# A new order of all five engines in a period of an attention and pooling kernel, with a fixed PSUM bank for each step

## The chip, the cores and the metric

The kernel runs on one core of one Trainium2 chip. The metric is device microseconds (us) of one execution; lower is better. Engines are named as in the profile: PE is TensorE, DVE is VectorE, ACT is ScalarE, POOL is GpSimd, SP is SyncE, which here only issues DMAs.

## The reference

The input `x` and a side input have 8 batches of 256 rows and 256 columns, in float32. Two layers with residuals follow each other:

```python
# layer 1: 16 heads of 16; keys and values from x; each row of side is also its own key and value
query = side + b_self;  key = [x + b_prev ; side + b_self];  value = [x ; side]
q, k, v = query @ Wq + bq, key @ Wk + bk, value @ Wv + bv
score = [ q.k_prev * s, masked beyond seq_len ; q.k_self * s ]      # 256 scores and one more
w = softmax(score)
x1 = x + (w_prev @ v_prev + w_self * v_self) @ Wo + bo
# layer 2: every row pools over the rows that its kind of mask allows
scores = tanh(x1 @ W1 + b1) @ v
p = softmax(where(mask, scores, -1e30))
out = x1 + (p @ x1) / count(mask)
```

## The kernel before, in words

Every float32 product with a weight is made of three products of float32r parts (`hi x hi`, `hi x lo`, `lo x hi`). So most results leave a PSUM bank twice: ACT copies the high part, DVE subtracts it to get the low part, and only then is the bank free.

The work is a software pipeline over batches. `period(n)` is written for each engine by hand, and each engine runs its own list in order; semaphores alone tie the lists together. In period n, PE works on four batches:

- batch n+1: transposes of side (`TS`, `side_transposed`) and x (`TX`, `x_transposed`), queries (`Q`), two halves of the keys (`K0`, `K1`), self values (`VS`), self scores (`SS`), values (`V`).
- batch n: eight maximum scores (`score_for_max`, two heads each, into `ps_max`), from which DVE takes row maxima (`max_of`), and the first exp scores.
- batch n-1: the other exp scores (`score_for_exp` into `ps_exp`), whose exponentials ACT writes (`exps`), four products of these with the values (`pv`, `PV0` to `PV3`), copied to `o_sb` by ACT, and the transposes back to natural order (`naturals`, `NAT0`, `NAT1`). DVE makes denominators and numerators of them (`denominators`: `den`, `rden`, `num`), and POOL multiplies (`attention`: `attn`).
- batch n-2: the transpose of attention (`AT`), the output product (`WO`), to which DVE adds the residual (`add_residual`: `x1`), the transpose of x1 (`X1T`), the hidden product of the pooling (`Z`, `pool_hidden`), its scores (`SB`), masked by DVE (`masked_scores`), exponentiated by ACT (`pool_exps`: `pool_p`), transposed (`PT`), and the pooled product (`PO`, `pooled`).

`ps_max` and `ps_exp` hold one score block each (two banks of PSUM each): a maximum score waits for the maximum before it (`max_found`), an exp score for the exponentials before it (`p_ready`). The other steps share four banks of `ps_any`. `shared_banks` walks `USES` (lines 43 to 67) and hands the banks out in rotation, in the order of use; `take_bank` (L1022) makes PE wait until the bank's last reader is done.

The row maxima reach the exp scores through a chain of small steps: DVE negates and splits them (`group_max`), PE transposes them (`max_to_rows`, `MT0` and `MT1` for heads 0 to 7 and 8 to 15), ACT copies the rows (`max_rows_copy`: `mt_sb`), and SP places them into `q_rows` by DMA (`place_max`, L335). Exp score 0 waits for group 0 and exp score 4 for group 1. Queries and keys take a longer way: they are spilled to DRAM (`spill_q`, `spill_k`) and read back by rows (`place_q`, `place_k`, in two groups); maximum score 0 of the next batch waits for group 0 of both.

In a period of before, PE's list has eight slots. Each has one maximum score, one exp score and, in every second one, a `pv`; the other steps stand between the slots. Lines 1214 to 1272 have PE's list, 629 to 677 ACT's, 931 to 976 DVE's, 474 to 487 POOL's and 384 to 400 SP's. SP's list is also hand-made: loads of x and side two batches ahead, spills and placements of batch n+1, and the residual's second load of x. Before the first period, batch 0 and the side, x and queries of batch 1 are prepared.

## Time and profile before

| | us |
|---|---|
| median of 3 runs | 306.69 |
| lowest and highest | 303.89, 310.06 |
| the profiled execution, its own time | 307.28 |
| its span, first to last instruction | 305.5 |

The profiled execution has busy shares of its span of 78% on PE, 58% on DVE, 50% on ACT and 21% on POOL. A busy share counts a matmul from its start to its modelled end, and those overlap, so start-to-start distances tell what a step takes on PE. DMA queues moved 35.57 MB at a mean of 116 GB/s. A row of waits names the waiting engine, the tile it works on, the engine and line that released it, and the time. PEclk is the clock granted to PE, 1.00 at 2.4 GHz and 0.50 at 1.2 GHz.

### The profile page before, as it was taken

The numbers are of one execution on the slowest core, as the hardware profiler recorded it, in microseconds if no ns is written. First come the engines' busy times: TensorE is split into PE (matmuls) and PEld (weight loads), VectorE is DVE, ScalarE is ACT, GpSimd is POOL, SyncE is SP. The second block draws the span as 40 slices with busy tenths as digits, with TensorE's granted clock in tenths as the row PEclk, the third lists the DMA queues.
The fourth block names the chain that finished last, engine by engine and source line by source line (L and its number), as shares of the span: only waits on it lengthen the run. The fifth ranks groups of instructions, "written<-read, shape, count | busy, mean of one in ns | idle before, by whom it ended". The sixth has DMA issues, their size and how long they took to land.

```text
span 305.5 us, 5479 instructions
## 1 busy us (share of the span) xinstructions
PE 238.5 (78%) x1988; PEld 180.8 (59%) x1988; DVE 178.4 (58%) x367; ACT 152.5 (50%) x281; POOL 64.8 (21%) x80
## 2 busy tenths in 40 slices
PE   2667487798888988898889888888898788586433
PEld 1657366566665767576757675766576546264323
DVE  3763547656766577657765776576658486214431
ACT  4133114566655656565656565656565274553220
POOL 9400100030151034103410341034104111411400
PEclk9978779799999999999999999999999797779957
DMA  6459615834952854285426542833274110200100
GB/s 164 139 195 208 185 68 146 171 106 163 199 165 101 185 134 141 100 194 128 139 98 176 149 141 92 190 71 124 101 189 79 36 39 2 72 0 0 36 1 34
DMA packets 28283, 35.57 MB, mean 116 GB/s; under 512 B 4440, under 2 KB 24672, under 8 KB 28256
## 3 DMA queue, kind: packets, MB, share of 16 engines
q1 hardware_dynamic: 27616, 33.12, 40.9%
q0 software_dynamic: 640, 2.10, 2.0%
q8 instruction: 16, 0.26, 0.4%
q14 instruction: 11, 0.09, 0.1%
HBM read 20.26 MB, written 14.69 MB: 114 GB/s over the span
## 4 chain that ended last, share of the span: by engine, by line
PE 56%; DVE 15%; issue 11%; ACT 9%; DMA 5%; SPq 2%; POOL 1%; ACTq 0%; DVEq 0%; POOLq 0%
PE ps_any L1013 14%; PE ps_any L1056 9%; PE ps_max L1094 7%; PE ps_any L1120 5%; PE ps_any L1019 5%; PE ps_any L1190 3%; PE ps_exp L1108 3%; PE ps_any L1136 3%; DMA q_rows<-mt_sb 2%; PE ps_any L1167 2%; ACT pool_p L620 2%; DVE s_max L828 2%; DVE prod L814 2%; PE ps_any L1175 2%; ACT q_full L523 2%
## 5 line engine op out<-in xcount | busy, mean ns | idle before, releaser
L828 DVE TENSOR_REDUCE s_max<-ps_max 128x4 f32<-128x1024 f32 x64 | 78.0, 1219 | 37.5 <-PE ps_max L1094 37.4
L542 ACT ACTIVATE pt<-ps_exp 128x1024 f32<-128x1024 f32 x64 | 65.5, 1024 | 52.3 <-PE ps_exp L1108 51.8
L1094 PE MATMUL ps_max<-k_rows,q_rows 49*128 49x256 f32 x256 | 33.1, 338 | 10.0 <-DVE s_max L828 7.5
L1120 PE MATMUL ps_any<-pt,v_aug 128*32 128x256 f32 x512 | 36.3, 403 | 0.3 <-ACT pt L542 0.3
L437 POOL TENSOR_TENSOR attn<-num,rden 128x256 f32<-128x256 f32 x16 | 9.6, 623 | 113.7 <-DVE rden L871 113.7
L1108 PE MATMUL ps_exp<-q_rows,k_rows 51*128 51x256 f32 x256 | 27.9, 296 | 6.4 <-DMA q_rows<-mt_sb 5.8
L1094 PEld LDWEIGHTS ps_max<-k_rows,q_rows 49*128 49x128 f32 x256 | 19.8, 190 | 22.0 <-DVE s_max L828 10.3
L1108 PEld LDWEIGHTS ps_exp<-q_rows,k_rows 51*128 51x128 f32 x256 | 20.4, 192 | 8.8 <-DMA q_rows<-mt_sb 7.1
L423 POOL TENSOR_TENSOR q_lo<-q_full,q_hi 128x512 fp32r<-128x512 f32 x7 | 8.9, 1274 | 74.9 <-ACT q_hi L528 74.9
L1013 PE MATMUL ps_any<-w_hi,in_hi 128*128 128x256 f32 x64 | 21.2, 331 | 3.0 <-DVE w_lo L710 2.6
L1120 PEld LDWEIGHTS ps_any<-pt,v_aug 128*32 128x32 f32 x512 | 13.8, 112 | 11.1 <-issue 2.1
L1013 PE MATMUL ps_any<-w_lo,in_hi 128*128 128x256 f32 x64 | 18.5, 290 | 0.0
L1013 PE MATMUL ps_any<-w_hi,in_lo 128*128 128x256 f32 x64 | 18.5, 289 | 0.0
L429 POOL TENSOR_TENSOR x_lo<-x,x_hi 128x512 fp32r<-128x512 f32 x8 | 10.4, 1304 | 31.6 <-ACT x_hi L597 31.6
L535 ACT ACTIVATE k_hi<-ps_any,bqk_col 128x256 fp32r<-128x256 f32 x16 | 7.6, 473 | 17.9 <-PE ps_any L1056 17.9
L1013 PEld LDWEIGHTS ps_any<-w_hi,in_hi 128*128 128x128 f32 x64 | 12.6, 196 | 6.6 <-issue 5.5
L1013 PE MATMUL ps_any<-w_hi,at_hi 128*128 128x256 f32 x32 | 10.9, 340 | 5.1 <-DVE at_lo L875 5.1
L1056 PE MATMUL ps_any<-in_hi,w_hi 128*128 128x512 f32 x32 | 14.8, 461 | 0.0
L1190 PE MATMUL ps_any<-x_hi,pool_pt_hi 128*128 128x256 f32 x32 | 10.3, 323 | 5.5 <-ACT v_aug L583 3.4
L795 DVE TENSOR_TENSOR in_lo<-ps_any,in_hi 128x512 fp32r<-128x512 f32 x8 | 5.5, 692 | 14.7 <-ACT in_hi L496 14.7
L548 ACT ACTIVATE o_sb<-ps_any 128x256 f32<-128x256 f32 x32 | 12.3, 384 | 3.3 <-PE ps_any L1120 3.3
L1056 PE MATMUL ps_any<-in_hi,w_lo 128*128 128x512 f32 x32 | 13.8, 431 | 0.0
(136 smaller groups left out, 535.8 us busy)
## 6 DMA issues: line engine op xcount, KB each, us to landing
q_rows<-q_spill SPq DMA_DIRECT2D x32, 192.0 KB, 4.3
k_rows<-k_spill SPq DMA_DIRECT2D x32, 192.0 KB
q_spill<-q_hi SPq DMA_DIRECT2D x16, 256.0 KB, 2.5
k_spill<-k_hi SPq DMA_DIRECT2D x16, 256.0 KB, 2.5
s_sb<-in_fside_BxSxS SPq DMA_DIRECT2D x8, 256.0 KB, 6.2
x_sb<-in_x SPq DMA_DIRECT2D x8, 256.0 KB, 5.9
q_spill<-q_lo SPq DMA_DIRECT2D x8, 256.0 KB, 2.7
k_spill<-k_lo SPq DMA_DIRECT2D x8, 256.0 KB, 2.1
```

The source lines that it names most:

```text
L429: nc.gpsimd.tensor_tensor(x1_lo[:], x1[:], x1_hi[:].bitcast(F32), ALU.subtract).then_inc(x1_lo_done, 1)
L437: nc.gpsimd.tensor_tensor(attn[:, t].rearrange("p (h d) -> p h d", d=DH), num[:, t].rearrange("p (h d) -> p h d", d=DH), rden[:, t].unsque ...
L542: nc.scalar.activation(pt[:, 2 * j % 8:2 * j % 8 + 2], ps_exp[:], ACT.Exp).then_inc(p_ready, 1)
L548: nc.scalar.activation(o_sb[:, g], bank_of(f"PV{g}", b)[:, 0], ACT.Copy).then_inc(pv_copied, 1)
L828: nc.vector.tensor_reduce(s_max[:, j // MJ, :, j % MJ, :], ps_max[:], AX.X, ALU.max).then_inc(max_found, 1)
L1013: last = pe.matmul(out_of[:, m], lhs, rhs, start=(j == 0), stop=(j == len(terms) - 1))
L1019: last = pe.transpose(out_of[:, kb, P * t:P * t + P], src[:, t, P * kb:P * kb + P], ident[:])
L1056: last = pe.matmul(bank.rearrange("p w s -> p (w s)"), (w_hi, w_lo)[c][:, 1, kb, P * m:P * m + P], (in_hi, in_lo)[a][:, kb].rearrange("p w ...
L1094: last = pe.matmul(ps_max[:, e, t], q_rows[b % 2][rows, j, P * t:P * t + P], k_rows[b % 2][rows, j, :], start=True, stop=True)
L1108: last = pe.matmul(ps_exp[:, e, t], k_rows[b % 2][rows, j, P * t:P * t + P], q_rows[b % 2][rows, j, :], start=True, stop=True)
L1120: last = pe.matmul(bank[32 * c:32 * c + 32, 0, :], v_aug[b % 2][:, t, h, :], pt[:, h % 8, t, :], start=(t == 0), stop=(t == KB - 1), skip_ ...
L1190: last = pe.matmul(bank[:, t], p[:, kb, P * t:P * t + P], a[:, kb, :], start=(j == 0), stop=(j == len(terms) - 1))
```

## The change

No instruction and no operand changes; the order of the five lists and the assignment of banks do. The steps of one batch also move between periods:

- `USES` has an explicit bank per step, and `shared_banks` follows a list of first uses and then the table. The table's order is PE's new order.
- PE: the output product of n-2 comes right behind maximum score 1. Attention's transpose moves from the period n+2 of a batch n to its period n+1, behind maximum score 7; side is transposed for batch n+2 in place of n+1, late in the period. `pv` 1 and `pv` 2 stand back to back behind exp score 6. One key half stands behind exp score 4, the other behind exp score 5 and the transpose of x1. The naturals come before maximum score 6 in place of behind 7, and exp score 2 of a batch moves to the end of its own period. Self values, naturals and pooled product are split into halves by argument; self values have `pv` 3 between their halves.
- DVE: products and low keys come before maximum 4 in place of behind it; denominators come between maxima 5 and 6; the side's low part is for batch n+2, and attention's low part ends the list.
- ACT: the order follows PE's; the copy of the second group of maxima rows ends the list of period n, ahead of exps 2 of batch n.
- POOL: attention and residual are for batch n-1, behind the x1 low part; the store comes last.
- SP: the loads are issued a period earlier, and the second group of maxima rows is placed behind both groups of the next batch's rows of q and k. The residual's load stands between these groups.

In the diff, removed lines of the lists of ACT, DVE and PE are left out (they stand above), as are the splits into halves.

```diff
 USES = [
...
+    ("MT1", -1, 2, "mt_copied", 2, 2),
+    ("PV0", -1, 0, "pv_copied", 4, 1),
+    ("TX", 1, 2, "xt_lo", 1, 1),
+    ("Q", 1, 1, "q_full_done", 1, 1),
+    ("WO", -2, 2, "x1_done", 1, 1),
+    ("K0", 1, 3, "k_lo", 2, 1),
+    ("X1T", -2, 0, "x1t_lo", 1, 1),
+    ("K1", 1, 1, "k_lo", 2, 2),
+    ("PV1", -1, 2, "pv_copied", 4, 2),
+    ("PV2", -1, 0, "pv_copied", 4, 3),
+    ("MT0", 0, 3, "mt_copied", 2, 1),
+    ("Z", -2, 1, "tanh_done", 1, 1),
+    ("SS", 1, 2, "ss_copied", 1, 1),
+    ("SB", -2, 1, "masked_done", 2, 2),
+    ("VS", 1, 3, "vs_copied", 1, 1),
+    ("PV3", -1, 2, "pv_copied", 4, 4),
+    ("NAT0", -1, 1, "num_done", 2, 1),
+    ("NAT1", -1, 0, "num_done", 2, 2),
+    ("PT", -2, 2, "pt_lo", 1, 1),
+    ("TS", 2, 3, "st_lo", 1, 1),
+    ("V", 1, 0, "v_copied", 1, 1),
+    ("AT", -1, 1, "at_lo", 1, 1),
+    ("PO", -2, 3, "out_done", 1, 1),
 ]

+FIRST_USES = [("TS", 0), ("TX", 0), ("Q", 0), ("K0", 0), ("K1", 0), ("VS", 0), ("SS", 0), ("V", 0),
+              ("TS", 1), ("TX", 1), ("Q", 1)]
+
 
 def shared_banks():
 
-    free, last, found = [None] * BANKS, -1, {}
-    for period in range(-1, NB + 3):
-        for step, offset, reader, per, done in USES:
-            if not 0 <= period + offset < NB:
-                continue
-            last = (last + 1) % BANKS
-            found[step, period + offset] = (last, free[last], len(found))
-            free[last] = (reader, (period + offset) * per + done)
+    row = {use[0]: use[2:] for use in USES}
+    order = FIRST_USES + [(step, period + offset) for period in range(-1, NB + 4) for step, offset, *_ in USES]
+    free, found = [None] * BANKS, {}
+    for step, b in order:
+        if not 0 <= b < NB or (step, b) in found:
+            continue
+        bank, reader, per, done = row[step]
+        found[step, b] = (bank, free[bank], len(found))
+        free[bank] = (reader, b * per + done)
     return found
...
-            for n in range(B + 1):
-                if live(n + 2):
+            for n in range(B + 2):
+                if 2 <= n + 2 < B:
                     load(n + 2)
+                if 1 <= n < B:
+                    spill_q(n)
+                    spill_k(n)
+                if live(n - 1):
+                    place_max(n - 1, 0)
+                if 1 <= n < B:
+                    place_q(n, 0)
+                    place_k(n, 0)
+                if live(n - 2):
+                    load_residual(n - 2)
+                if 1 <= n < B:
+                    place_q(n, 1)
+                    place_k(n, 1)
                 if live(n - 1):
                     place_max(n - 1, 1)
-                if live(n + 1):
-                    spill_q(n + 1)
-                    spill_k(n + 1)
-                if live(n):
-                    place_max(n, 0)
-                if live(n + 1):
-                    place_q(n + 1, 0)
-                    place_k(n + 1, 0)
-                    place_q(n + 1, 1)
-                    place_k(n + 1, 1)
-                if live(n - 1):
-                    load_residual(n - 1)
...
-            for n in range(B + 3):
-                if live(n - 2):
-                    attention(n - 2)
-                    residual(n - 2)
-                if n == 0:
-                    queries_lo(1)
-                elif live(n + 1):
+            for n in range(B + 2):
+                if 1 <= n + 1 < B:
                     queries_lo(n + 1)
-                if live(n - 3):
-                    store(n - 3)
                 if live(n - 1):
                     self_values(n - 1)
                 if live(n - 2):
                     x1_low(n - 2)
+                if live(n - 1):
+                    attention(n - 1)
+                    residual(n - 1)
+                if live(n - 2):
+                    store(n - 2)
             pool.wait_ge(out_stored, 16 * B)
...
         def _(act):
...
             def period(n):
+                if live(n - 1):
+                    exps(n - 1, 2)
+                    pv_copy(n - 1, 0)
+                if 2 <= n + 1 < B:
+                    x_hi(n + 1)
+                if live(n - 1):
+                    exps(n - 1, 3)
+                if 2 <= n + 1 < B:
+                    queries(n + 1)
+                if live(n - 1):
+                    exps(n - 1, 4)
+                    exps(n - 1, 5)
+                if live(n - 2):
+                    x1t_high(n - 2)
+                if 1 <= n + 1 < B:
+                    keys_hi(n + 1)
+                if live(n - 2):
+                    x1_high(n - 2)
+                if live(n - 1):
+                    exps(n - 1, 6)
+                if live(n):
+                    max_rows_copy(n, 0)
+                if live(n - 1):
+                    pv_copy(n - 1, 1)
+                    self_exps(n - 1)
+                if live(n - 2):
+                    tanh(n - 2)
+                if live(n - 1):
+                    exps(n - 1, 7)
+                if 1 <= n + 1 < B:
+                    self_scores_copy(n + 1)
+                if live(n - 1):
+                    pv_copy(n - 1, 2)
+                    pv_copy(n - 1, 3)
+                if live(n - 2):
+                    pool_exps(n - 2)
+                if 1 <= n + 1 < B:
+                    self_values_copy(n + 1)
+                if live(n):
+                    exps(n, 0)
+                if live(n - 2):
+                    pool_high(n - 2)
+                if 2 <= n + 2 < B:
+                    side_hi(n + 2)
+                if live(n):
+                    exps(n, 1)
+                if live(n - 1):
+                    attention_hi(n - 1)
+                if 1 <= n + 1 < B:
+                    values_copy(n + 1)
+                if live(n):
+                    max_rows_copy(n, 1)
 
...
         def _(dve):
...
             def period(n):
+                if live(n):
+                    max_of(n, 0)
+                if live(n - 3):
+                    result(n - 3)
+                if 2 <= n + 1 < B:
+                    x_lo(n + 1)
+                if live(n):
+                    max_of(n, 1)
+                if live(n - 1):
+                    self_args(n - 1)
+                if live(n):
+                    max_of(n, 2)
+                if live(n - 2):
+                    add_residual(n - 2)
+                if live(n):
+                    max_of(n, 3)
+                    group_max(n, 0)
+                if live(n - 2):
+                    x1t_low(n - 2)
+                if 1 <= n + 1 < B:
+                    products(n + 1)
+                    keys_lo(n + 1)
+                if n + 1 == 1:
+                    weight_lo(3)
+                if n + 1 == 1:
+                    output_bias()
+                if live(n):
+                    max_of(n, 4)
+                if live(n - 2):
+                    hide(n - 2)
+                    masked_scores(n - 2)
+                if live(n):
+                    max_of(n, 5)
+                if live(n - 1):
+                    denominators(n - 1)
+                if live(n):
+                    max_of(n, 6)
+                if live(n - 2):
+                    pool_low(n - 2)
+                if 2 <= n + 2 < B:
+                    side_lo(n + 2)
+                if live(n):
+                    max_of(n, 7)
+                    group_max(n, 1)
                 if n == 0:
+                    setup_pooling()
+                if live(n - 1):
+                    attention_lo(n - 1)
 
...
         def _(pe):
...
             def period(n):
+                if live(n):
+                    score_for_max(n, 0)
+                if live(n - 1):
+                    max_to_rows(n - 1, 1)
+                    pv(n - 1, 0)
+                if 2 <= n + 1 < B:
+                    x_transposed(n + 1)
+                    queries(n + 1)
+                if live(n):
+                    score_for_max(n, 1)
+                if live(n - 1):
+                    score_for_exp(n - 1, 3)
+                if live(n - 2):
+                    output_product(n - 2)
+                if live(n):
+                    score_for_max(n, 2)
+                if live(n - 1):
+                    score_for_exp(n - 1, 4)
+                if 1 <= n + 1 < B:
+                    keys(n + 1, 0)
+                if live(n):
+                    score_for_max(n, 3)
+                if live(n - 1):
+                    score_for_exp(n - 1, 5)
+                if live(n - 2):
+                    x1_transposed(n - 2)
+                if 1 <= n + 1 < B:
+                    keys(n + 1, 1)
+                if n + 1 == 1:
                     bv_product()
+                if live(n):
+                    score_for_max(n, 4)
+                if live(n - 1):
+                    score_for_exp(n - 1, 6)
+                    pv(n - 1, 1)
+                    pv(n - 1, 2)
+                if live(n):
+                    max_to_rows(n, 0)
+                if live(n - 2):
+                    pool_hidden(n - 2)
+                if live(n - 1):
+                    score_for_exp(n - 1, 7)
+                if live(n):
+                    score_for_max(n, 5)
+                if 1 <= n + 1 < B:
+                    self_scores(n + 1)
+                if live(n - 2):
+                    pool_scores(n - 2)
+                if 1 <= n + 1 < B:
+                    self_values(n + 1, 0)
+                if live(n - 1):
+                    pv(n - 1, 3)
+                if 1 <= n + 1 < B:
+                    self_values(n + 1, 1)
+                if live(n - 1):
+                    naturals(n - 1, 0)
+                    naturals(n - 1, 1)
+                if live(n):
+                    score_for_exp(n, 0)
+                    score_for_max(n, 6)
+                if live(n - 2):
+                    pool_transposed(n - 2)
+                if 2 <= n + 2 < B:
+                    side_transposed(n + 2)
+                if 1 <= n + 1 < B:
+                    values(n + 1, 0)
+                if live(n):
+                    score_for_exp(n, 1)
+                    score_for_max(n, 7)
+                if live(n - 1):
+                    attention_transposed(n - 1)
+                if 1 <= n + 1 < B:
+                    values(n + 1, 1)
+                if live(n - 2):
+                    pooled(n - 2, 0)
+                    pooled(n - 2, 1)
+                if live(n):
+                    score_for_exp(n, 2)
```

## Rows read from the trace of the kernel before

**Rows 1.** The page: span; busy us of each engine, with share and instructions.

```profile
span 305.5 us, 5479 instructions
...
PE 238.5 (78%) x1988; PEld 180.8 (59%) x1988; DVE 178.4 (58%) x367; ACT 152.5 (50%) x281; POOL 64.8 (21%) x80
```

**Rows 2.** Stretches: A:B us, length, busy us by engine, PEclk, DMA share, GB/s.

```profile
55.00:79.80 24.80, 22.79 (x204) 16.38 (x204) 15.46 (x31) 14.73 (x25) 2.44 (x3) 0.93 0.58 152
79.80:110.30 30.50, 26.82 (x246) 20.67 (x246) 19.90 (x40) 18.36 (x35) 7.01 (x9) 1.00 0.68 166
202.30:232.90 30.60, 26.77 (x247) 20.60 (x246) 20.34 (x40) 18.43 (x34) 6.92 (x10) 1.00 0.45 123
232.90:258.60 25.70, 20.87 (x183) 14.71 (x182) 17.08 (x34) 13.67 (x24) 5.15 (x8) 0.87 0.07 23
258.60:285.20 26.60, 18.01 (x146) 11.86 (x146) 9.21 (x25) 11.80 (x22) 8.77 (x11) 0.87 0.06 21
285.20:305.50 20.30, 8.38 (x40) 6.43 (x40) 5.04 (x12) 3.50 (x8) 1.98 (x2) 0.73 0.08 27
```

**Rows 3.** Waits of TensorE, 173.5 to 204.2: us in total, times, longest.

```profile
PE ps_any L1167 <- DVE k_lo L822: 1.0, 1, 1.0
PE ps_any L1013 <- DVE at_lo L875: 0.8, 1, 0.8
PE ps_any L1019 <- ACT pool_p L620: 0.8, 1, 0.8
PE ps_any L1190 <- ACT v_aug L583: 0.7, 1, 0.7
```

**Rows 4.** Timeline of TensorE in that period: start us, duration us.

```profile
183.19 0.48 PE L1056 MATMUL ps_any<-in_hi,w_hi 128*128 128x512 f32 x1
...
186.16 0.50 PE L1094 MATMUL ps_max<-k_rows,q_rows 49*128 49x256 f32 x4
186.50 0.40 PE L1108 MATMUL ps_exp<-q_rows,k_rows 51*128 51x256 f32 x4
186.83 1.07 PE L1120 MATMUL ps_any<-pt,v_aug 128*32 128x256 f32 x16
187.83 0.28 PE L1128 MATMUL ps_any<-ident,neg_max 128*32 128x128 f32 x1
...
191.05 0.47 PE L1013 MATMUL ps_any<-w_hi,in_hi 128*128 128x256 f32 x1
...
192.66 0.96 PE L1075 MATMUL ps_any<-headsum,prod 128*128 128x8 f32 x8
193.55 0.50 PE L1094 MATMUL ps_max<-k_rows,q_rows 49*128 49x256 f32 x4
```

**Rows 5.** Timeline of VectorE, same columns.

```profile
186.71 1.23 DVE L828 TENSOR_REDUCE s_max<-ps_max 128x4 f32<-128x1024 f32 x1 [1.32 <-PE ps_max L1094]
187.85 0.87 DVE L814 SCALAR_TENSOR_TENSOR prod<-ps_any,bqk_col,q_full 128x256 f32<-128x256 f32 x2
188.63 0.87 DVE L822 SCALAR_TENSOR_TENSOR k_lo<-ps_any,bqk_col,k_hi 128x256 fp32r<-128x256 f32 x2
```

**Rows 6.** Timeline of ScalarE, same columns.

```profile
186.94 1.02 ACT L542 ACTIVATE pt<-ps_exp 128x1024 f32<-128x1024 f32 x1 [0.20 <-PE ps_exp L1108]
```

**Rows 7.** Chain of waits near 260 us: start us, us, what.

```profile
260.50 0.26 ACT mt_sb L554
...
261.43 2.99 DMA q_rows<-mt_sb
```

**Rows 8.** Chain of waits, period 0: start us, us, what.

```profile
46.11 0.80 DVE k_lo L822 x2
...
50.64 4.28 DMA k_rows<-k_spill
```

**Rows 9.** A stretch of period 7, and a row of its chain of waits.

```profile
240.00:244.00 4.00, 4.00 (x28) 3.17 (x20) 0.58 (x1) 0.69 (x2) 0.00 (x0) 0.59 0.00 0
...
240.53 2.87 PE ps_any L1013 x12
```

More of the change, by code:

```diff
@@ L629, in period @@
             def period(n):
-                nxt, now, prv, old = n + 1, n, n - 1, n - 2
-                if live(prv):
-                    exps(prv, 2)
-                    pv_copy(prv, 0)
-                    max_rows_copy(prv, 1)
-                if live(nxt) and n > 0:
-                    side_hi(nxt)
-                    x_hi(nxt)
-                if live(prv):
-                    self_exps(prv)
-                    exps(prv, 3)
-                if live(nxt) and n > 0:
-                    queries(nxt)
@@ L674, in period @@
-                if live(now):
-                    exps(now, 1)
-                if live(nxt):
-                    values_copy(nxt)
+                if live(n - 1):
[10 more added lines that the diff above has]
+                    exps(n - 1, 5)
@@ L692, in _ @@
             queries(1)
-            for n in range(B + 3):
+            for n in range(B + 2):
                 period(n)
@@ L996, in _ @@
                 period(n)
-                if n == 0:
-                    setup_pooling()
         @block.tensor
@@ L1077, in self_scores, with values @@
                 last.then_inc(ss_ready, 1)
-            def values(b, halves):
-                bank = take_bank("V", b) if 0 in halves else bank_of("V", b)
-                last = products(bank, in_hi[:, :, X], in_lo[:, :, X], 2, False, halves)
-                if 1 in halves:
+            def values(b, m):
+                bank = take_bank("V", b) if m == 0 else bank_of("V", b)
+                last = products(bank, in_hi[:, :, X], in_lo[:, :, X], 2, False, (m,))
+                if m == 1:
                     last.then_inc(v_ready, 1)
@@ L1258, in period @@
-                if live(nxt):
-                    self_values(nxt)
-                    self_scores(nxt)
-                scores(6)
-                if live(nxt):
-                    values(nxt, (0,))
-                if live(old):
-                    pool_transposed(old)
-                scores(7)
-                if live(prv):
-                    naturals(prv)
-                if live(nxt):
-                    values(nxt, (1,))
-                if live(old):
-                    pooled(old)
+                if live(n):
+                    score_for_max(n, 0)
@@ L1286, in _ @@
             queries(1)
-            for n in range(B + 3):
+            for n in range(B + 2):
                 period(n)
```

194 lines of the change are left out of this document (31 added, 163 removed).

## The prediction

> **What bounds the kernel now.** I read the page's totals first: TensorE is busy for 238.5 of 305.5 us, no other engine for over 59% [rows 1]. An average says little here, so the next view is the table of stretches, cut where the first maximum score of each batch starts [rows 2]. From 79.8 to 232.9 us there are five like periods; of them the first and the last are shown, and each takes 30.5 to 30.7 us with TensorE busy for 26.8, at a granted clock of 1.00. VectorE is busy for about 20 us of such a period, ScalarE for 18. So TensorE's in-order stream sets the period, and 3.9 us of it are waits. The waits of one such period [rows 3] name the four that make 3.3 of it: the pooling hidden product behind the low part of the keys (1.0), the output product behind `at_lo` (0.8), the pooling transpose behind `pool_p` (0.8), the pooled product behind the value copy (0.7). None is bandwidth; each is a consumer placed too soon after its producer. The two periods at the end are of another kind: 25.7 and 26.6 us for only 20.9 and 18.0 us of matmuls, at 0.87 of the clock.
>
> **What moves.** No instruction is added or removed (loops that ran one period longer had nothing live there), the DMAs are the same in number and size. So TensorE's 26.8 us per period are the floor, and the question is what still waits. I lay the new order of one middle period out from durations of rows, with zero at the end of the period's first maximum score.
>
> TensorE, start to start [rows 4]: a maximum score 0.34, an exp score 0.33, a value product (`pv`) 1.0, twelve matmuls 1.6, a self score 0.89, keys 1.5 a half. VectorE: a maximum 1.23, two products 0.8, two low keys 0.8 [rows 5]. ScalarE: an exp 1.02 [rows 6]. Shorter steps go by their own durations in the same period (a copy 0.4 or 0.6, masking 1.65, pooling exps 1.15, denominators 1.1, GpSimd's multiply 0.6 a half). After an engine ends, the next starts within 0.2.
>
> *First third.* The transpose of the maxima ends at 0.1, `pv` 0 at 1.1, x transposed 1.7, queries 3.3. ScalarE now copies the maxima rows ahead of exp 2, so it stands until TensorE has made that transpose; exp 2, the copy of `pv` 0 and `x_hi` queue behind, and exp 2 ends at 1.8. Exp score 3, which waits for it, comes at 3.6: 1.8 us in hand. The output product starts at 3.9: `at_hi` and `at_lo` were made in the period before, and its bank needs only `x_lo` (3.5). The 0.8 wait goes. Exp 3 is queued before the query copy, so `q_hi` ends at 6.5 instead of 3.6, and the spill of q starts 2.9 us later on SP; keys are spilled only at 11, so nothing waits.
>
> *Middle.* Max score 2 at 5.5, exp score 4 at 5.9, keys 0 to 7.7, scores to 8.3, x1 transposed: VectorE takes maximum 2 (6.0 to 7.2) and then adds the residual, done 7.9, before TensorE asks at 8.3. Keys 1 to 10.2. VectorE now does products and low keys ahead of maximum 4: low keys end at 12.4, maximum 4 at 13.7. Behind maximum 4 stands max score 5, which TensorE reaches at 14.2, because two value products (2.0), the maxima's transpose and the pooling hidden product (0.85) lie between. The hidden product starts at 13.0 against 12.4: the 1.0 wait goes, with only 0.6 us of cover.
>
> *Last third.* Self scores from 14.5, pooling scores 15.4, half the self values to 16.6, `pv` 3 (exp 7 done 15.6) to 17.6, the other half to 18.4. `pv` 3's copy ends at 18.1; the naturals wait for it with 0.3 in hand. VectorE masks until 17.5, maximum 5 until 18.8 (max score 6 asks at 19.6), denominators 19.3 to 20.4, maximum 6 until 21.7 (max score 7 asks at 22.2). The pooling transpose asks at 19.9, `pool_p` is done at 19.2. GpSimd multiplies attention at 20.7 to 21.3 and the transpose comes at 22.5. The pooled product asks at 23.9; its bank is freed by the low side part at 23.3. ScalarE's value copy no longer gates it. The 0.8 and 0.7 go too, and the period closes at about 26.1.
>
> **Queues passed.** SP: the maxima rows of group 1 are issued behind the row placements of group 1 of the next batch, which end at about 21, five us before those rows exist. From the copy's end to landing such rows took 3.7 us [rows 7], and exp score 4 asks 5.2 us after the copy. Group 0 of the next batch is issued from 14.8 on; its longest landing in a row is 4.3 us [rows 8], so it is there by 22 for a use at 26. GpSimd: the store now stands last and holds the queue until VectorE's result 2.2 us into the next period; `q_lo` behind it is due at 6.5. The x load moves a period earlier: half a megabyte of traffic sooner in the first period, when SP is idle.
>
> **The sum, against the profiled execution's own 307.28 us** (its span 305.5 and 1.8 around it; the median is 306.69, so 0.6 lower).
> - Five middle periods: 5 x 3.9 = 19.2 us of waits. All vanish on paper; since four covers are under 0.7 us I leave 0.25 a period: -18.0.
> - Start: in period 0 the low keys no longer stand behind maximum 4, so the key spill, and the 4.3 us landing that the first score of batch 1 waits for [rows 8], start about 3 us sooner; VectorE's constants, which stay, hold the first maximum of batch 1. On paper batch 1 starts at 52.2 in place of 55.0 and batch 2 at 75.4 in place of 79.8, 4.4 sooner; the half clock that stands in the gaps of period 0 may keep 1 of it: -3.4.
> - Period 7: on paper 20.8 instead of 25.7; exp score 4 is limited by the maxima rows (4.2) and TensorE by exps. TensorE ran at half clock in such a gap: twelve matmuls took 2.87 where 1.6 is usual [rows 4, 9]. That and 0.5 for hand-overs kept: -3.2.
> - Period 8: from the start of the exps: maxima rows 4.2, exps 4 and 5 to 7.0, score 6 and two `pv` to 9.3, hidden product 10.2, exp 7 to 11.7, `pv` 3 and its copy 13.2, naturals 14.3, denominators and attention 16.4, its transpose and split 18.4, output product of the last batch at 18.8; before, 26.6. Batch 7's attention no longer stands behind batch 6's pooled product or a period boundary. Keeping 2.3 for half clock and hand-overs: -5.5.
> - The last 20 us [rows 2] are one batch's chain, untouched: 0.
>
> 307.3 - 18.0 - 3.4 - 3.2 - 5.5 = 277.2. I predict 277.
>
> **The rivals.**
> *A new wait on a short chain (0.13).* `pv` 3, copy, naturals, denominators, attention, its transpose now follow inside one period, with 0.3 to 1.2 us in hand at each link. If hand-overs cost 1.5 to 2 us a period over seven periods, 12 us come back: 289. For it: two transposes and a product wait on others' in-order streams; against: the same rows were used for every link.
> *Rows land late (0.10).* If the maxima rows or keys take the 4.3 us of the key rows or more, because loads and spills now meet them, exp score 4 waits about 1 us a period: 284. For it: DMA's share rises from 0.45 to 0.68 of 30.6 us to 0.52 to 0.78 of 26.8 [rows 2]; against: five us in hand.
> *It moves nothing (0.03).* The waits removed come back one for one at the shared banks: 307.
> *Slower: the clock (0.04).* All 23 uses share four banks. If TensorE waits briefly before many of them and its clock falls to 1.2 GHz, the 26.8 us of a period grow by up to 26.8; the half-clock row [rows 9] shows the price, 2.87 for 1.6. It decides from 37 us lost, one and a half of the seven periods at half clock: about 315. Against: at 3.9 us of waits a period the clock stood at 1.00 [rows 2], and there are fewer now.
> The Trainium skill ("TensorE: Matmul & The Clock Gate", the section on psum-queue depth-cycling) says that a kernel which cycled through its banks let TensorE idle briefly between groups, and that its clock went back and forth between two levels. By that rule the period would be longer than the layout; by the five middle periods it doesn't bind here.
>
> **The numbers.** The forecast (267 to 283) gets 0.70; its low end takes all waits off and the paper gains of the edges: 19.2 + 4.4 + 4.9 + 7.9 = 36.4, and 0.6 us a period from start-to-start sums, 3 more: 268. The range 267 to 289 takes in both delays. What a measurement can tell from no change is about 2%, 6 us. Faster 0.92, same 0.04, slower 0.04.
>
> **What would show it.** In the changed profile the middle periods should be 26.3 to 27.3 us with under 1 us of TensorE waits; `k_lo`, `at_lo`, `pool_p` and `v_aug` gone from its releasers; the first score of batch 1 near 52 us; 21 to 23 and 19 to 21 us for periods 7 and 8. Wrong would be: new waits on `num` or `attn` (first rival), on `q_rows<-mt_sb` in middle periods (second), a granted clock below 1.00 there (fourth).

## The result and the profile after

| us | before | changed | 
|---|---|---|
| median of 4 runs | 306.64 | 277.16 |
| lowest, highest | 303.89, 310.06 | 273.28, 279.59 |
| the profiled execution | 307.28 | 273.28 |
| its span | 305.5 | 271.5 |

The ratio of changed to before is 0.902, interval 0.888 to 0.916. A second set of 4 runs gave 278.36 in the median and a ratio of 0.898 (0.886 to 0.910). I had predicted 277. The single profiled execution of the changed kernel is 4 us faster than the median, and with it the comparison by parts below is 34.0 us and not 29.5; the section on why says where executions differ.

The page of the changed kernel, span and engines. TensorE has the same matmuls in 34 us less:

```profile
span 271.5 us, 5479 instructions
...
PE 230.6 (85%) x1988; PEld 179.3 (66%) x1988; DVE 181.8 (67%) x367; ACT 148.5 (55%) x281; POOL 64.7 (24%) x80
```

Stretches of the changed kernel, cut again where the first maximum score of a batch starts (columns as in [rows 2]; period 0, period 1, the first and last of the five middle ones, period 7, period 8 to the last batch's output product, the last batch's chain):

```profile
33.30:56.80 23.50, 18.33 (x100) 14.27 (x99) 13.66 (x20) 6.63 (x12) 1.27 (x1) 0.78 0.63 170
56.80:79.90 23.10, 21.47 (x206) 15.93 (x208) 16.94 (x42) 14.57 (x27) 4.22 (x6) 1.00 0.55 159
79.90:106.90 27.00, 26.07 (x250) 20.57 (x248) 21.02 (x42) 18.12 (x35) 6.98 (x8) 1.00 0.68 162
185.20:210.90 25.70, 25.70 (x246) 20.14 (x244) 19.84 (x39) 17.25 (x33) 6.98 (x8) 1.00 0.51 147
210.90:232.30 21.40, 17.47 (x184) 12.17 (x180) 17.40 (x33) 13.39 (x24) 5.61 (x7) 1.00 0.08 27
232.30:251.70 19.40, 14.43 (x142) 9.67 (x141) 8.09 (x22) 11.24 (x21) 5.61 (x7) 1.00 0.10 30
251.70:271.50 19.80, 7.85 (x40) 6.23 (x40) 7.09 (x14) 3.38 (x8) 2.74 (x3) 0.68 0.08 27
```

Of the five middle periods the first took 27.0 us, the last 25.8 and those between 26.0 to 26.2. TensorE is busy to the last tenth in all but the first; the 3.9 us of waits per period are gone. Periods 7 and 8 lose 4.4 and 7.1 us, and the tail after them hardly changes (20.3, now 19.8).

The waits of TensorE in all five middle periods of the changed kernel (us in total, times, longest) are this single one, once, in the first of them; nothing took the place of the four of [rows 3]:

```profile
PE ps_any L1139 <- DVE neg_max L850: 0.9, 1, 0.9
```

| part, from the starts of the maximum scores | before | changed | difference | forecast |
|---|---|---|---|---|
| before the first score | 31.4 | 33.3 | +1.9 | 0 |
| periods 0 and 1 | 48.4 | 46.6 | -1.7 | -3.4 |
| five middle periods | 153.2 | 131.0 | -22.1 | -18.0 |
| period 7 | 25.7 | 21.3 | -4.4 | -3.2 |
| period 8, up to the last output product | 26.6 | 19.5 | -7.1 | -5.5 |
| the last batch's chain | 20.3 | 19.8 | -0.5 | 0 |

### The profile page after: what moved, and what is told of

It reads as the page before. It is cut to its first block, busy times and chain, and to the rows that moved or that the text cites. A ratio compares the mean times of both kernels' runs of the same rounds, so it can differ in the third digit from the quotient of the medians.

```text
span 271.5 us, 5479 instructions
## 1 busy us (share of the span) xinstructions
PE 230.6 (85%) x1988; PEld 179.3 (66%) x1988; DVE 181.8 (67%) x367; ACT 148.5 (55%) x281; POOL 64.7 (24%) x80
## 4 chain that ended last, share of the span: by engine, by line
PE 74%; DVE 14%; issue 5%; ACT 4%; DMA 2%; POOL 1%; SPq 0%; DVEq 0%; ACTq 0%; POOLq 0%
PE ps_any L1022 17%; PE ps_any L1131 10%; PE ps_any L1065 9%; PE ps_max L1105 8%; PE ps_exp L1119 7%; PE ps_any L1028 7%; DVE s_max L836 5%; PE ps_any L1202 4%; PE ps_any L1086 3%; PE ps_any L1146 3%; PE ps_any L1177 2%; ACT pt L546 2%; PE ps_max L1214 1%; PE ps_any L1185 1%; DVE bin_parts L724 1%
## 5 line engine op out<-in xcount | busy, mean ns | idle before, releaser
L1105 PE MATMUL ps_max<-k_rows,q_rows 49*128 49x256 f32 x256 | 29.7, 311 | 8.0 <-DVE s_max L836 7.9
L1131 PE MATMUL ps_any<-pt,v_aug 128*32 128x256 f32 x512 | 32.6, 383 | 0.6 <-ACT pt L546 0.6
L1119 PE MATMUL ps_exp<-q_rows,k_rows 51*128 51x256 f32 x256 | 29.6, 310 | 2.8 <-ACT pt L546 2.6
L1105 PEld LDWEIGHTS ps_max<-k_rows,q_rows 49*128 49x128 f32 x256 | 19.8, 189 | 17.3 <-DVE s_max L836 9.2
L1022 PE MATMUL ps_any<-w_hi,in_hi 128*128 128x256 f32 x64 | 22.6, 354 | 2.6 <-DVE w_lo L718 2.6
L420 POOL TENSOR_TENSOR vs_p<-v_self,p_self 128x256 f32<-128x256 f32 x16 | 9.6, 619 | 52.2 <-ACT p_self L566 52.2
L1022 PE MATMUL ps_any<-w_lo,in_hi 128*128 128x256 f32 x64 | 19.2, 300 | 0.0
L913 DVE TENSOR_TENSOR masked<-hidden,ps_any 128x256 f32<-128x256 f32 x16 | 6.7, 416 | 17.7 <-PE ps_any L1185 17.7
L1022 PEld LDWEIGHTS ps_any<-w_hi,in_hi 128*128 128x128 f32 x64 | 13.4, 210 | 6.0 <-DVE k_lo L830 3.0
L459 POOL DMA_DIRECT2D out<-o_out x8 | 6.1, 764 | 34.7 <-DVE o_out L934 34.7
L1065 PE MATMUL ps_any<-in_lo,w_hi 128*128 128x512 f32 x32 | 13.6, 425 | 0.0
L1022 PEld LDWEIGHTS ps_any<-w_lo,in_hi 128*128 128x128 f32 x64 | 13.5, 211 | 0.1
```

The costliest lines, as they stand in the source:

```text
L420: last = nc.gpsimd.tensor_tensor(vs_p[:, t].rearrange("p (h d) -> p h d", d=DH), v_self[:, b % 2, t].rearrange("p (h d) -> p h d", d=DH), ...
L1022: last = pe.matmul(out_of[:, m], lhs, rhs, start=(j == 0), stop=(j == len(terms) - 1))
L1065: last = pe.matmul(bank.rearrange("p w s -> p (w s)"), (w_hi, w_lo)[c][:, 1, kb, P * m:P * m + P], (in_hi, in_lo)[a][:, kb].rearrange("p w ...
L1105: last = pe.matmul(ps_max[:, e, t], q_rows[b % 2][rows, j, P * t:P * t + P], k_rows[b % 2][rows, j, :], start=True, stop=True)
L1119: last = pe.matmul(ps_exp[:, e, t], k_rows[b % 2][rows, j, P * t:P * t + P], q_rows[b % 2][rows, j, :], start=True, stop=True)
L1131: last = pe.matmul(bank[32 * c:32 * c + 32, 0, :], v_aug[b % 2][:, t, h, :], pt[:, h % 8, t, :], start=(t == 0), stop=(t == KB - 1), skip_ ...
```

## The experiments

The theory under test: TensorE's in-order stream is the bound, and each step has just the cover that a layout by hand gives it. If so, each edit's effect can be worked out beforehand to a few tenths. The measure is a middle period of the changed kernel, 26.04 us from first score to first score (106.93 to 132.97, for one); in its two profiles five of the ten middle periods have that length, nine lie between 25.8 and 26.2, and one took 27.0. The rival: the gain, or the bound, lies elsewhere. Each edit is made to the changed kernel unless it says otherwise. The whole times come from two or four runs and carry the edges of the program with them, which vary by several us from run to run, so the length of a middle period decides and not the whole time.

### Low keys back behind maximum 4

```diff
+                if live(n):
+                    max_of(n, 4)
                 if 1 <= n + 1 < B:
                     products(n + 1)
                     keys_lo(n + 1)
 ...
-                if live(n):
-                    max_of(n, 4)
```

> VectorE's products and low keys go back behind maximum 4 in every period; all else is the changed kernel. Theory (the hand layout): TensorE's stream is the bound, each step has the cover that the layout gives it. Low keys then end 1.23 us later, at 13.6 of the period, where the transpose of the maxima asks at 12.9 and the pooling hidden product at 13.0: about 0.7 us of wait returns, middle periods of 26.9 us in place of 26.2. Rival (the gain comes from elsewhere, the slack is wider than the layout says): middle periods stay at 26.2.

A stretch of one middle period, and its wait:

```profile
106.60:133.50 26.90, 26.40 (x252) 20.68 (x250) 20.61 (x41) 17.77 (x34) 7.13 (x8) 1.00 0.59 160
```

```profile
PE ps_any L1139 <- DVE k_lo L830: 0.4, 1, 0.4
```

26.84 us from score to score, 0.8 more than 26.04: the theory's number. The profile puts down only 0.4 of it as a wait. The last of the five middle periods took 28.4 us, at a granted clock of 0.94 and with the same wait. The median of two runs was 280.4.

### Attention's transpose back into the later period

```diff
-                if live(n - 1):
-                    attention_transposed(n - 1)
 ...
                     queries(n + 1)
+                if live(n - 2):
+                    attention_transposed(n - 2)
 # ACT: attention_hi(n - 2) before exps 3; DVE: attention_lo(n - 2) behind maximum 1
```

> Attention's transpose goes back into period n+2 of its batch, between the queries and maximum score 1, its high and low parts with it (ahead of exps 3, behind maximum 1); the output product stays in slot 1. Theory: the high part ends at 4.7, VectorE is in maximum 1 until 5.6 and has the low part at 6.3, where the output product would ask at 4.4: 1.9 us a period, middle periods of 28.1 us, some 12 us in all. Rival (the place of the transpose is neutral, other waits set the pace): 26.2.

```profile
102.10:130.00 27.90, 26.13 (x252) 20.58 (x249) 20.42 (x40) 17.98 (x34) 7.12 (x8) 1.00 0.56 154
```

```profile
PE ps_any L1022 <- DVE at_lo L883: 9.0, 5, 1.9
```

27.9, 28.1 and 27.7 us in the three periods at full clock, 1.9 to 2.0 over the same periods of the changed kernel, and a wait of up to 1.9 us in each of the five. The other two took 29.4 and 29.75 us at a granted clock of 0.94, so half clock came in two of five periods with waits of this size. The two runs took 290.5 and 302.8. So the output product in slot 1 lives on the earlier transpose: with it placed late, the five middle periods take 142.8 us, and 11.8 of the 22.1 us gained there are lost.

### The rotation of banks with the new order

```diff
-    free, found = [None] * BANKS, {}
+    free, last, found = [None] * BANKS, -1, {}
 ...
-        bank, reader, per, done = row[step]
+        _, reader, per, done = row[step]
+        last = bank = (last + 1) % BANKS
```

> The new order of all engines with the banks handed out in rotation as before. Theory: the rotation makes the pooling scores wait for the copy of the third value product (about 0.8 us) and the queries for the result of the pooled product (0.5), so middle periods of 27.0 to 27.5 us. Rival (the fixed table is only another way to write the same waits): 26.2.

The waits of its middle periods (us in total, times, longest):

```profile
PE ps_any L1186 <- ACT o_sb L553: 2.8, 5, 0.6
PE ps_any L1023 <- DVE o_out L935: 1.2, 4, 0.3
```

27.4 us a period, 1.37 more. Both waits are where the theory put them: the pooling scores behind a copy to `o_sb`, the queries behind `o_out`. The fixed table is worth 1.4 us a period, 5.3 us over the five middle periods; the order alone brings the larger part, 16.9 of the 22.1 us there. The two runs took 282.0 and 286.0.

### The output product back in slot 2

```diff
-                if live(n - 2):
-                    output_product(n - 2)
                 if live(n):
                     score_for_max(n, 2)
                 if live(n - 1):
                     score_for_exp(n - 1, 4)
+                if live(n - 2):
+                    output_product(n - 2)
```

> The output product goes back to slot 2, behind maximum score 2 and exp score 4; attention's transpose stays a period early. Theory: in slot 1 the product also covers maximum 1; without it maximum score 2 asks at 3.9 and gets its bank at 4.9, 0.9 to 1.0 us of wait, middle periods of 27.0. Rival (only the early transpose counts): 26.0.

```profile
PE ps_max L1105 <- DVE s_max L836: 5.4, 5, 1.1
```

27.02 us, as expected: 1.1 us of wait for a maximum in each of five periods. The wait stands at maximum score 2, which the 1.6 us of the product had covered. The clock stayed at 1.00 in all five. Here the shown wait (1.09) is not smaller than what the period lost (0.98). The two runs took 278.4 and 278.0, no more than the changed kernel on the same chip (275.1 to 280.0), though the five middle periods took 4.8 us more: a total of two runs cannot show such an effect.

### The two value products apart

```diff
                     pv(n - 1, 1)
-                    pv(n - 1, 2)
 ...
                     score_for_max(n, 5)
+                if live(n - 1):
+                    pv(n - 1, 2)
```

> The two value products no longer stand back to back: the third goes behind maximum score 5, its bank use behind the pooling hidden product's. Theory: the hidden product then asks at 12.0 for the low keys of 12.4, and the maxima's transpose at 11.9: 0.5 us of wait, middle periods of 26.5. Rival (their place is neutral): 26.0.

Timeline of TensorE in one middle period (start, duration), the last value product before the maxima's transpose, that transpose, the hidden product and the exp score behind it:

```profile
121.06 1.07 PE L1131 MATMUL ps_any<-pt,v_aug 128*32 128x256 f32 x16
122.06 0.28 PE L1139 MATMUL ps_any<-ident,neg_max 128*32 128x128 f32 x1
122.38 0.33 PE L1177 MATMUL ps_any<-x1t_hi,w_hi 128*64 128x256 f32 x1
...
123.33 0.50 PE L1119 MATMUL ps_exp<-q_rows,k_rows 51*128 51x256 f32 x4
```

26.55 us, 0.5 more, as expected. No wait stands beside any of these rows, yet the hidden product starts 0.32 after the transpose's start, where the changed kernel has 0.05 (120.23 to 120.28): the modelled end of the transpose (0.28 long) covers the gap. VectorE's row shows what it waited for, the low keys, which end at 122.33:

```profile
121.46 0.87 DVE L830 SCALAR_TENSOR_TENSOR k_lo<-ps_any,bqk_col,k_hi 128x256 fp32r<-128x256 f32 x2
```

That is 0.27 us where I expected 0.5 of such a wait. The rest is two things that I had not reckoned with: the two value products take 1.00 each when apart and 1.86 together when back to back (118.37 to 120.23 in the changed kernel), 0.14 more, and the exp score behind the hidden product starts 0.09 later, right behind the exponentials that end at 123.29. So the size was met in part by luck. The two runs took 284.2 and 281.9.

### Less work for TensorE

```diff
+                parts = ((0, 0), (0, 1)) if n == 2 else ((0, 0), (0, 1), (1, 0))
                 for m in halves:
-                    terms = [(kb, a, c) for kb in range(KB) for a, c in ((0, 0), (0, 1), (1, 0))]
+                    terms = [(kb, a, c) for kb in range(KB) for a, c in parts]
```

> Left out: the product of the inputs' low part with the weights' high part, in values and self values alone; 16 fewer matmuls of 0.118 us a batch... counted per half two of six, so 8 a batch, 0.95 us of TensorE. Theory (TensorE's stream is the bound with no waits): middle periods fall by nearly that, from 26.0 to about 25.2 (the pooled product's bank then waits 0.2). Rival (another engine or a chain of hand-overs sets 26.0 by now): unchanged.

```profile
105.80:131.00 25.20, 25.20 (x242) 19.62 (x240) 20.01 (x41) 17.65 (x34) 7.14 (x8) 1.00 0.62 170
```

25.23 us: 0.81 of 0.95 us of removed matmuls come out of the period. TensorE bounds it, and VectorE or ScalarE would allow at least that much less. The two runs took 269.2 and 274.0; part of the work is left out, so these are no times of a usable kernel.

### More work for VectorE

```diff
+                if n > 0 and live(n):
+                    for i in range(2):
+                        nc.vector.tensor_tensor(pad[:, i], side_of[:], side_of[:], ALU.add)
                 if live(n):
                     max_of(n, 4)
```

> Two useless VectorE additions (128x512, about 0.6 us each) ahead of maximum 4 in each period from 1. VectorE is idle for 5 of 26 us, so by an average nothing happens. Theory: at this place the layout gives 0.6 us in hand before maximum score 5 asks, so about 0.6 of the 1.2 us comes through, middle periods of 26.6 to 26.8. Rival 1 (VectorE has slack everywhere): 26.0. Rival 2 (VectorE's chain is the bound): 27.2.

```profile
PE ps_max L1109 <- DVE s_max L837: 1.8, 5, 0.4
```

26.67 us: of 1.2 us put in, 0.6 came through (0.4 shown as a wait), though VectorE is idle for 5.0 us of each period even with the additions in it. What counts is the cover at the place. Both runs took 282.2 to 282.3.

### One part alone, in the kernel before

```diff
-                if live(now):
-                    max_of(now, 4)
                 if live(nxt):
                     products(nxt)
                     keys_lo(nxt)
+                if live(now):
+                    max_of(now, 4)
```

> The kernel before with one part of the change alone: VectorE's products and low keys ahead of maximum 4. Theory: the 1.0 us wait of the pooling hidden product goes, and maximum score 5 then waits 0.3 for maximum 4, so 0.7 us a period is kept: middle periods of 29.9 in place of 30.6, and period 0 about 1 us shorter since the keys are spilled sooner; 5 us in all. Rival (a wait removed alone reappears whole at the next step of the chain): 30.6.

Its waits in the middle periods, those that changed:

```profile
PE ps_any L1013 <- DVE at_lo L875: 4.5, 5, 1.1
...
PE ps_max L1094 <- DVE s_max L828: 2.0, 5, 0.4
```

29.8 us a period, 0.8 less than before. `k_lo` is gone from the list (5.2 us over five periods before), a wait for a maximum of 0.4 took its place, as worked out, and the wait for `at_lo` grew from 3.6 to 4.5 us. Four runs: median 298.55, ratio 0.967 (0.955 to 0.979). By the medians that is 9 us where I expected 5. By the two profiled executions it is 7.2 us (307.28 and 300.12): the middle gives 3.8, where 3.5 was expected, periods 0 and 1 give 2.1, and 1.3 lie at the other edges, where executions of one kernel differ by more than that. This one move of many has 3.8 of the 22.1 us of the middle by itself.

Four of the moves were thus taken back or made alone, and the bank table with them. The waits for `pool_p` and `v_aug`, 1.5 us a period before, were not put back one at a time, and neither were the new orders of SP and POOL: that their moves took these waits away is read from the list of waits and not tested.

### The start: VectorE's odd jobs out of the way of maximum 4

The part that fell clearly short was periods 0 and 1. The chain of waits of the changed kernel there (start, duration, what):

```profile
42.79 0.88 DVE prod L822 x2
43.67 0.78 DVE k_lo L830 x2
44.45 0.67 DVE w_lo L718 x2
45.12 0.33 DVE bias_out L798
45.45 1.15 DVE s_max L836
...
46.64 0.50 PE ps_max L1105 x4
47.14 1.60 PE ps_any L1086 x8
48.74 2.76 PE ps_any L1022 x12
```

In period 0 the low part of Wo and the output bias stand between the low keys and maximum 4. Maximum score 5 waits 2.24 us for maximum 4, and what follows runs at a granted clock of 0.50, 1.2 GHz: the twelve matmuls of the self values take 2.76 us where 1.6 is usual [rows 4].

```profile
48.00:52.00 4.00, 4.00 (x20) 3.78 (x22) 0.41 (x1) 0.66 (x2) 0.00 (x0) 0.50 1.00 221
```

```diff
-                if n + 1 == 1:
-                    weight_lo(3)
-                if n + 1 == 1:
-                    output_bias()
 ...
                     max_of(n, 5)
+                if n == 0:
+                    output_bias()
 ...
                     max_of(n, 6)
+                if n == 0:
+                    weight_lo(3)
```

> Only period 0 differs: the low part of Wo and the output bias leave VectorE's queue ahead of maximum 4 and go behind maxima 6 and 5. Theory: the 2.24 us wait of maximum score 5, after which TensorE ran at half clock, becomes 1.2 us; the clock stays at 1.00 in 47 to 54 us and period 0 takes about 20.5 us in place of 23.4, the kernel 3 us less. Rival 1 (half clock comes anyway): 1.0 us less. Rival 2 (the keys' rows from DRAM set the start of batch 1): nothing.

> The first new start again (the low part of Wo and the output bias behind maxima 6 and 5). Theory: period 0 of 21 us, 2.4 less than the changed kernel's, the rest equal; 2 to 3 us in the time. Rival: the half clock moves to another stretch and the time is the same within noise.

| | first set | second set | period 0 in the profiles |
|---|---|---|---|
| new start, median of 4 | 275.28 | 269.96 | 21.1, 21.2 |
| its ratio to before | 0.897 (0.867 to 0.927) | 0.878 (0.866 to 0.891) | |
| changed kernel, median of 4 | 277.16 (not side by side) | 278.36 | 23.5, 21.8 |
| its ratio to before | 0.902 (0.888 to 0.916) | 0.898 (0.886 to 0.910) | |

Side by side on one chip, in the second set, the new start is 8.4 us faster by medians; over the eight runs of each, the medians are 272.8 and 277.2. The intervals of the ratios overlap, and the profiles of the second set warn against reading 8.4 us as the edit's work. Their spans differ by 8.7 us (275.4 and 266.7), but only 0.6 of it lies in period 0. The middle periods are equal, 3.1 us lie ahead of the first score and 5.0 in period 7 and behind it, where the edit changes nothing. So a gain is likely, its size is not settled, and by medians this is the fastest version that does all the work.

The theory fell in one point: the wait of maximum score 5 did shrink to 1.2 us, but the clock did not stay. A stretch of the second profile of the new start, behind that score:

```profile
45.60:49.60 4.00, 4.00 (x25) 3.55 (x24) 0.96 (x3) 1.62 (x3) 0.00 (x0) 0.57 0.91 209
```

Half clock came in every profile of these versions, behind a wait of 2.2 us or of 1.2, and in a shorter or a longer stretch. Where it was long, period 0 took 23.4 to 23.5 us (the first profile of the changed kernel and those of four experiments, one of which had the wait elsewhere, for the low keys), and two more profiles have 22.9 and 23.1; where it was short, 21.8 (the second profile and that with the late transpose) and, with the new start, 21.1 and 21.2. So by the profiles the edit itself is worth 0.6 us, and up to 2.4 if it also makes the long stretch rarer, which two profiles cannot show. Rival 1, half clock in any case and 1.0 us less, was nearer than my theory. Most of the 4.4 us between the medians of eight has no cause shown here.

### The start with keys in the gaps

```diff
+                if n == 0:
+                    keys(1, 0)
                 if live(n):
                     score_for_max(n, 1)
+                if n == 0:
+                    keys(1, 1)
 # and bv_product() behind exp score 4; both key halves leave their old places in period 0
```

> On top of the first new start, TensorE makes the two key halves of batch 1 behind maximum scores 0 and 1 of period 0, in the time that it waits for VectorE's maxima, and the bias product behind maximum score 2. Theory: three waits of 1.2 to 1.3 us are filled with 3 us of matmuls, and TensorE keeps its clock; period 0 of 18.5 to 19.5 us. Rival (VectorE, with eight maxima and 5 us of other work, bounds period 0): 20.5 or more.

```profile
PE ps_max L1105 <- DVE s_max L836: 2.8, 3, 1.4
PE ps_any L1139 <- DVE k_lo L830: 1.0, 1, 1.0
```

21.4 us: the rival. These are the waits of period 0. Those for maxima fell to 2.8 us from 4.1 and 3.9 in the two profiles of the new start, but the one for the low keys grew from 0.3 to 1.0, so 3.8 us of waits are left of 4.2 to 4.4, and the granted clock of the period was 0.76 in place of 0.84. The gaps were moved more than filled, so this does not tell what the clock does when they are filled. Median 274.6, no better than the new start. Whether VectorE or the clock holds period 0 at 21 us stays open.

### The changed kernel again

> The changed kernel as it is, to be compared with the two starts on the same chip: period 0 of about 23.4 us, middle periods of 26.0.

```profile
34.70:56.50 21.80, 16.72 (x98) 12.62 (x98) 13.71 (x20) 6.58 (x12) 1.27 (x1) 0.84 0.60 162
209.70:233.80 24.10, 20.15 (x184) 13.98 (x180) 18.24 (x35) 13.43 (x24) 5.62 (x7) 0.87 0.08 25
```

Three middle periods were 26.04 us to the hundredth, the first 26.16 and the last 25.76; the 0.9 us wait in the first middle period of the first profile did not come again, which makes 1.0 us. The other differences from the first profile are at the edges: the first score at 34.7 in place of 33.3, period 0 of 21.8 us in place of 23.5, period 7 of 24.1 us at a clock of 0.87 in place of 21.3 at 1.00, with the same five waits in it, and period 8 of 21.5 us at 0.91 in place of 19.5 at 1.00.

## Why the prediction was right

**Bound and floor.** Right in kind: all four waits of [rows 3] went, and with none left a change of TensorE's work or of one cover shows at once. The size was off by 4 us: -18.0 forecast, -22.1 measured. The step behind it was to call TensorE's 26.8 busy us the floor: the periods took 26.0, below the 26.3 to 27.3 that I had named as the sign. The 19.2 us of idle time understate what the waits cost, since the drawn end of the last matmul before a wait hides its first part. In a run of twelve the starts are 0.12 us apart and each is drawn 0.28 long, so by an estimate from these rows up to 0.16 us a wait is drawn as busy; before, a period had six waits, the four of [rows 3] and two of 0.4 and 0.2. Four experiments show the same: 0.8 us lost for a shown 0.4, 1.37 for 0.8, 0.6 for 0.4, 0.5 for none. Two do not (0.98 lost for 1.09, 1.9 for 1.8), and part of the 0.8 us is not from waits at all, as the 0.14 us that two value products save back to back. My start-to-start sum, 26.1, had the floor; I used it only for the low end of the range. The 0.25 us a period kept for hand-overs was not needed either.

**First third.** Right. Exp score 3 was not late behind ScalarE's wait for the transposed maxima, and the later spill of q cost nothing. The two experiments on this third (1.9 and 1.0 us) gave the layout's numbers.

**Middle.** Right: there is cover of some 0.6 us before the hidden product, since low keys 1.2 us later cost 0.8, and of 0.6 before maximum score 5, as VectorE's extra work measured it.

**Last third.** The short chain from `pv` 3 to attention's transpose held with no wait in any middle period; the first rival did not come. Its narrowest link, 0.3 us, was not tested by itself.

**Queues.** Right: no wait for `q_rows<-mt_sb` in a middle period, so the second rival did not come. In period 8 the maxima rows do set the pace, as forecast; from the copy's start at 233.01 to their landing it is 3.5 us:

```profile
233.01 0.28 ACT mt_sb L558
...
233.30 0.61 SPq L344
...
233.96 2.51 DMA q_rows<-mt_sb
...
236.51 0.52 PE ps_exp L1119 x4
```

**Start.** This step failed: -1.7 in place of -3.4, or +0.2 with the stretch before it. The low keys ended 11.2 us behind the first score in place of 15.5 [rows 8], and the wait for their rows went. But the prediction took the key spill for what sets the start of batch 1, and once it was early, maximum 4 was late: it stood behind the low keys and two jobs of 1.0 us in all. TensorE waited 2.24 us for it, and from 47 to 54 us it ran at half clock. Batch 1 started 23.5 us after batch 0, as before, where the paper had 20.8, and its first score came at 56.8 and not near 52. Nearly the whole gain lies in period 1, 23.1 us in place of 24.8, where the paper had 23.2.

The 1.9 us ahead of the first score are the pace of TensorE too. All of them lie in the same sixteen, twelve and eight matmuls; the first two groups are shown, before and then changed:

```profile
12.96 2.15 PE ps_max L1201 x16
15.11 4.28 PE ps_any L1056 x12
...
12.95 3.57 PE ps_max L1214 x16
16.52 4.57 PE ps_any L1065 x12
```

Over all profiles the first score comes at 31.4 to 35.3 us, and at 27.5 in one, where 1.7 us are VectorE's: a small cast ahead of these matmuls took 1.4 us in place of 3.2.

**Periods 7 and 8.** The layout without its allowances (20.8 and 18.8) was nearly met, 21.3 and 19.5, where the clock stood at 1.00 in both; in the second profile they took 24.1 and 21.5 at 0.87 and 0.91, outside the 21 to 23 and 19 to 21 that I had named. My allowance for half clock was the price of one product, and there is either none to pay or more than that.

**The total.** That 277 fits the median to 0.2 us is luck. The sum was made against the profiled execution, and the one profiled after the change took 273.3, so there it was 4 us off: the middle gave 4.1 us more than forecast, periods 7 and 8 gave 2.8 more, the start and the stretch ahead of it took 3.6. The other executions of that set took 277.0 to 279.6; the second profile shows how the edges can cost that much more.

**The clock as a rival.** It did not come: the middle stands at 1.00 before and after. It came in no middle period of the output product back in slot 2 either, with a wait of 1.1 us in each. The Trainium skill ("TensorE: Matmul & The Clock Gate", the sections on HAM oscillation and on psum-queue depth-cycling) says that waits between groups of matmuls can let the clock fall, so that the next group starts slow. The trace agrees in kind at the edges (a wait of 2.24 us, then 2.76 for 1.6) and with the late transpose (waits of 1.9 us, two of five periods at 0.94), and hardly any of it with short waits: the middle periods of the rotation, with waits of 0.6 and 0.3 us, took 27.0 to 27.4 us, and of those with the low keys behind maximum 4 one in five took 28.4 us at 0.94. The changed kernel, with no such waits, had none in two profiles. That the waits are the cause is read from this order of things and was not tested by itself.

## What to carry to other kernels

When one in-order engine sets the period and its waits are short, lay one period out by hand from start-to-start durations, write the cover beside each step, and move the producers with too little of it; here it foretold eight edits to within 0.2 us a period, one of them with only half of the cause right. Take the price of a wait from the length of the period, not from the idle time in the list of waits, which missed up to 0.6 us a period. At the edges of the program, where TensorE has gaps anyway, half clock comes and goes by the run; allow for its cost there as a range and not as a term. And when a step at the start is made earlier, ask what stands next in the same engine's list: here two small jobs behind it kept the gain from TensorE.

## What the runs showed of the hardware

A cost that I had not expected is that of a gap too short to be shown: starts 0.27 us later than need be, with no idle time in the profile, because matmul ends are modelled. And executions of one kernel differ by nearly 7 us (273.3 to 280.0) while most of its middle periods are equal to the hundredth. The two profiles of the changed kernel show where: 33.3 or 34.7 us before the first score, 23.5 or 21.8 us for period 0, 21.3 or 24.1 us for period 7, 19.5 or 21.5 for period 8. With the same waits in the same places, half clock was there or not, or lasted longer.

In the first 20 us the granted clock of the profile cannot be taken at its word. From 17 to 19.9 us of the first profile of the changed kernel it reads 1.00, but the matmuls there, 512 columns wide, start 0.43 us apart, where at 1.00 in a middle period the same ones start 0.23 apart (116.67 and 116.90). The start-to-start distance shows the pace; later on, as in the stretch of 48 to 52 us above, the clock column agrees with it.
